# The same steps in another order on five engines: a four-layer graph network over 32 batches

## The reference

```
h = relu(layernorm(x)); x = x + L0(h, adj)   # 8-head attention with q=k=v, then an MLP 256-1024-256 with gelu
h = relu(layernorm(x)); x = x + L1(h, adj)   # graph attention, 4 heads: weights exp(leaky_relu(s_i + t_j)), masked
h = relu(layernorm(x)); x = x + L2(h, adj)   # the same form, other weights
h = relu(layernorm(x)); x = x + L3(h, adj)   # 4-head attention with q, k, v and output projection, masked, diagonal open
```

## Time and profile before

| what | us |
|---|---|
| median of three runs (lowest, highest) | 4239.26 (4238.15, 4240.60) |
| the profiled execution itself | 4241.92 |
| its span, from the first to the last instruction | 4240.1 |
| PE busy | 4042.6 (95%) |
| DVE busy | 3223.4 (76%) |
| ACT busy | 2166.5 (51%) |
| POOL busy | 408.3 (10%) |
| mean granted TensorE clock, share of full | 0.988 |

### The profile page before, as it was taken

The page is one execution under the profiler, slowest core; times in us unless marked ns, Lnnn a source line. Parts: engine busy times, 40 slices in busy tenths (PEclk is TensorE's granted clock), DMA queues, the critical chain, the costliest instruction groups (busy, mean ns, idle before and its releaser), DMA issues.

```text
span 4240.1 us, 58963 instructions
## 1 busy us (share of the span) xinstructions
PE 4042.6 (95%) x22884; PEld 1929.7 (46%) x22884; DVE 3223.4 (76%) x6473; ACT 2166.5 (51%) x3361; POOL 408.3 (10%) x469
## 2 busy tenths in 40 slices
PE   5799999999999999999999999999999999999997
PEld 1344444444444444444444444444444444444443
DVE  5677778877778877777877777877778877788854
ACT  3454555544555554555544555544555544555532
POOL 0001011101011101110100110100110100110100
PEclk9999999999999999999999999999999999999998
DMA  3111111111111111111111111112111111211000
GB/s 99 29 42 50 56 37 49 34 53 51 56 36 51 31 53 52 56 36 51 31 52 54 56 35 51 31 51 56 56 32 54 31 51 56 56 31 46 21 31 31
DMA packets 212311, 193.90 MB, mean 46 GB/s; under 512 B 144448, under 2 KB 179008, under 8 KB 203584
## 3 DMA queue, kind: packets, MB, share of 16 engines
q1 hardware_dynamic: 212032, 190.12, 15.3%
HBM read 138.95 MB, written 17.56 MB: 37 GB/s over the span
## 4 chain that ended last, share of the span: by engine, by line
PE 90%; DVE 5%; ACT 4%; DMA 1%; issue 1%; SPq 0%; POOL 0%; POOLq 0%; ACTq 0%; DVEq 0%
PE O L477 12%; PE M L425 11%; PE M L438 10%; PE S L358 6%; PE S L524 6%; PE O L371 6%; PE M L491 6%; PE O L540 6%; PE M L449 6%; PE O L481 5%; PE M L502 3%; PE M L416 3%; PE M L582 3%; PE O L382 2%; ACT PP L625 2%; PE M L398 2%
## 5 line engine op out<-in xcount | busy, mean ns | idle before, releaser
L1014 DVE SCALAR_TENSOR_TENSOR PG<-g,tcg,mT 128x512 f32<-128x512 f32 x1024 | 691.2, 742 | 33.1 <-PE O L481 21.4
L625 ACT ACTIVATE PP<-S,reach 128x1024 f32<-128x1024 f32 x512 | 542.6, 1111 | 318.8 <-PE O L371 114.5
L906 DVE TENSOR_TENSOR PP<-PP,mT 128x1024 f32<-128x1024 f32 x512 | 597.3, 1218 | 16.5 <-ACT PP L625 16.0
L477 PE MATMUL O<-PG,V 128*32 128x512 f32 x4096 | 550.9, 602 | 18.5 <-DVE PG L1014 17.0
L425 PE MATMUL M<-hT,W 128*128 128x512 f32 x1024 | 460.6, 603 | 3.1 <-ACT hT L660 2.8
L438 PE MATMUL M<-W,H 128*128 128x256 f32 x2048 | 459.7, 378 | 0.0
L438 PEld LDWEIGHTS M<-W,H 128*128 128x128 f32 x2048 | 377.3, 189 | 71.7 <-issue 10.6
L1126 POOL TENSOR_SCALAR ve<-mv 128x4 f32<-128x4 f32 x192 | 97.8, 509 | 3197.4 <-DVE mv L864 3197.4
L358 PE MATMUL S<-hT 32*128 32x512 f32 x2048 | 301.3, 658 | 30.8 <-ACT PP L625 29.4
L739 ACT ACTIVATE PP<-S,sh 128x1024 f32<-128x1024 f32 x256 | 272.1, 1118 | 87.5 <-DVE Q L916 49.0
L603 ACT ACTIVATE V<-z,nb,rs 128x256 f32<-128x256 f32 x128 | 76.6, 602 | 467.4 <-DVE nb L896 467.4
(11 more groups left out here) (136 smaller groups left out, 5608.5 us busy)
## 6 DMA issues: line engine op xcount, KB each, us to landing
g<-t_rows SPq DMA_DIRECT2D x64, 1024.0 KB, 4.7
adj<-adj_in SPq DMA_DIRECT2D x32, 1024.0 KB, 5.5
x<-x_in SPq DMA_DIRECT2D x32, 512.0 KB, 4.0
z<-t_rows SPq DMA_DIRECT2D x64, 256.0 KB, 4.0
out<-x SPq DMA_DIRECT2D x32, 512.0 KB, 2.9
W<-w_in SPq DMA_DIRECT2D x1, 3072.0 KB, 13.0
mT<-z SPq DMA_TRANSPOSE x128, 2.5
m<-V SPq DMA_TRANSPOSE x128, 2.5
```

The source lines that it names most:

```text
L477: e.matmul(k.O[0][r:r + 32, :], s.V[:, jt, 64 * hh + 32 * v:64 * hh + 32 * v + 32], p[:, u, :], start=(jt == 0), stop=(jt == NT - 1))
L625: e.activation(p[:, 2 * pair:2 * pair + 2, :], k.S[:, 2 * pair:2 * pair + 2, :], ACT.Exp, bias=k.reach[:, 7:8], scale=SC0).then_inc(k.e0.s ...
L906: e.tensor_tensor(p[:, 2 * pair:2 * pair + 2, :], p[:, 2 * pair:2 * pair + 2, :], s.mT[:, jt:jt + 1, :].to_broadcast([128, 2, N]), ALU.mul ...
L1014: e.scalar_tensor_tensor(out=p[:, u, :], in0=s.T[hh], scalar=s.tcg[:, 1, hh, jt:jt + 1], in1=s.mT[:, jt, :], op0=ALU.max, op1=ALU.mult).th ...
```

## The change

All five lists are replaced. Each list still holds the same steps for the same batches, each once; no step is changed. Where the loop is cut differs: on PE the 28 steps from `b2r(·,0,2)` to `w2(·,3)`, which stood at the head of a pass, stand at the end of the pass before, with batch numbers shifted by one, so the sequence through that cut is as it was. Besides that, steps trade places. The diff, cut to the places spoken of below (the batch numbers of the removed and added lines differ by the shift):

```diff
--- before.py
+++ after.py
         do.tt(b3, 3, 0)
+        do.sc0(b1, 2)
         do.tt(b3, 3, 1)
-        do.sc0(b1, 2)
         do.b2r(b2, 1, 0)
-        do.b2r(b2, 1, 1)
         do.pv0(b1, 0)
         do.pv0(b1, 1)
+        do.b2r(b2, 1, 1)
+        do.b2r(b2, 1, 2)
         do.dn0(b1, 0)
-        do.b2r(b2, 1, 2)
         do.b2r(b2, 1, 3)
         do.sc0(b1, 3)
-        do.pv0(b1, 2)
         do.qk(b3, 0)
         do.qk(b3, 1)
         do.sc0(b1, 4)
+        do.pv0(b1, 2)
         do.pv0(b1, 3)
...
         do.dn0(b1, 1)
+        do.pv0(b1, 4)
         do.qk(b3, 3)
         do.vp(b3, 0)
         do.sc0(b1, 6)
-        do.pv0(b1, 4)
         do.sq3(b3, 0)
...
         do.sc3(b3, 0)
+        do.vp(b3, 1)
         do.tt(b2, 2, 0)
+        do.pv0(b1, 7)
+        do.dn0(b1, 3)
         do.tt(b2, 2, 1)
-        do.pv0(b1, 7)
-        do.vp(b3, 1)
-        do.dn0(b1, 3)
         do.sc3(b3, 1)
...
 def scalar_program(do):
...
+        do.vp(b3, 1)
         do.tt(b2, 2, 0)
-        do.tt(b2, 2, 1)
         do.sc3(b3, 0)
         do.out0(b1, 1)
-        do.vp(b3, 1)
+        do.tt(b2, 2, 1)
         do.sc3(b3, 1)
-        do.ln0(b0, 0)
         do.sc3(b3, 2)
...
+        do.w1(b1, 7)
+        do.ln0(b0, 0)
+        do.out3(b3, 1)
+        do.ln0(b0, 1)
+        do.ln0(b0, 2)
...
 def vector_program(do):
...
-        do.masks(b1, 1)
-        do.resid0(b2)
-        do.bst(b1, 1, 0)
-        do.bst(b1, 1, 1)
-        do.diag(b1)
...
-        do.zb(b1)
...
         do.wo(b4, 0)
+        do.diag(b1)
         do.wo(b4, 1)
...
         do.rc(b2, 1, 0)
+        do.b2r(b2, 1, 0)
         do.rc(b2, 1, 1)
-        do.b2r(b2, 1, 0)
         do.b2r(b2, 1, 1)
...
+        do.pa0(b1, 3)
+        do.sh3(b3)
+        do.zb(b1)
+        do.sc3(b3, 0)
...
+        do.sc3(b3, 1)
+        do.bst(b1, 2, 0)
+        do.pa3(b3, 0)
...
+        do.fin(b1, 0, 3)
+        do.pa3(b3, 1)
+        do.bag(b1, 2, 2)
+        do.bst(b1, 2, 3)
+        do.bag(b1, 2, 3)
+        do.pj(b2, 2, 0)
+        do.pj(b2, 2, 1)
+        do.sc3(b3, 2)
+        do.pj(b2, 2, 2)
+        do.nb(b1, 2)
...
 def gpsimd_program(do):
...
+        do.rs(b2, 0)
+        do.rs(b3, 3)
+        do.rs(b2, 1)
         do.gmax(b3, 1)
         do.rs(b4, 5)
         do.rs(b3, 4)
-        do.rs(b1, 0)
         do.rs(b2, 2)
         do.gmax(b3, 2)
-        do.rs(b1, 1)
-        do.rs(b2, 3)
...
 def sync_program(do):
...
-        do.loada(b1)
-        do.trow(b4, 2)
-        do.tbc(b4, 2)
...
+        do.trow(b3, 2)
+        do.tbc(b3, 2)
+        do.masks_t(b1, 0)
+        do.masks_t(b1, 1)
...
+        do.store(b4)
+        do.load(b0)
+        do.loada(b0)
```

More of the change, by code:

```diff
@@ L1382, in scalar_program @@
         do.lnz(b3, 3, 2)
+        do.qt(b1, 1)
         do.lnz(b3, 3, 3)
@@ L1390, in scalar_program @@
         do.sc0(b1, 4)
+        do.out0(b1, 0)
         do.qk(b3, 1)
@@ L1393, in scalar_program @@
         do.sc0(b1, 5)
-        do.out0(b1, 0)
+        do.qk(b3, 3)
         do.sq3(b3, 0)
-        do.lnz(b2, 2, 0)
-        do.qk(b3, 3)
-        do.lnz(b2, 2, 1)
         do.vp(b3, 0)
@@ L1529, in vector_program @@
         do.pa0(b1, 1)
-        do.bst(b2, 4, 1)
-        do.bag(b2, 4, 0)
+        do.fin(b2, 1, 1)
+        do.bst(b0, 0, 0)
+        do.bst(b0, 0, 1)
+        do.bst(b2, 4, 0)
         do.fin(b2, 1, 2)
         do.fin(b2, 1, 3)
-        do.bst(b0, 0, 0)
+        do.sc0(b1, 4)
+        do.bst(b2, 4, 1)
         do.bst(b2, 4, 2)
+        do.bag(b2, 4, 0)
         do.bag(b2, 4, 1)
@@ L1539, in vector_program @@
         do.bag(b2, 4, 3)
-        do.bag(b0, 0, 0)
[L1541 to L1544, removed]
+        do.sc0(b1, 5)
+        do.pa0(b1, 2)
+        do.sq3(b3, 0)
+        do.sc0(b1, 6)
+        do.nb(b2, 4)
+        do.sq3(b3, 1)
+        do.sc0(b1, 7)
+        do.pa0(b1, 3)
+        do.sh3(b3)
+        do.zb(b1)
+        do.sc3(b3, 0)
+        do.rc(b1, 0, 0)
+        do.b2r(b1, 0, 0)
+        do.rc(b1, 0, 1)
+        do.bag(b0, 0, 0)
+        do.fin(b1, 0, 0)
@@ new lines, in vector_program @@
+        do.sc3(b3, 1)
+        do.bst(b1, 2, 0)
+        do.pa3(b3, 0)
+        do.b2r(b1, 0, 1)
+        do.rc(b1, 0, 2)
+        do.bag(b1, 2, 0)
+        do.b2r(b1, 0, 2)
+        do.fin(b1, 0, 1)
+        do.fin(b1, 0, 2)
+        do.bst(b1, 2, 1)
+        do.rc(b1, 0, 3)
+        do.bag(b1, 2, 1)
+        do.b2r(b1, 0, 3)
+        do.bst(b1, 2, 2)
+        do.fin(b1, 0, 3)
[3 more added lines that the diff above has]
+        do.bag(b1, 2, 3)
+        do.pj(b2, 2, 0)
@@ L1545, in vector_program @@
+        do.pj(b2, 2, 1)
+        do.sc3(b3, 2)
+        do.pj(b2, 2, 2)
+        do.nb(b1, 2)
+        do.prep_b(b1)
+        do.prep_w(b1)
         do.bst(b0, 0, 2)
         do.bag(b0, 0, 1)
-        do.pa0(b1, 2)
+        do.pj(b2, 2, 3)
+        do.gmax(b2, 2)
+        do.sc3(b3, 3)
+        do.gprep(b2, 2)
+        do.pa3(b3, 2)
+        do.pa3(b3, 3)
+        do.masks(b0, 0)
+        do.bst(b0, 0, 3)
         do.bag(b0, 0, 2)
-        do.bst(b0, 0, 3)
-        do.sq3(b3, 0)
-        do.sc0(b1, 6)
@@ L1552, in vector_program @@
         do.bag(b0, 0, 3)
[L1553 to L1561, removed]
-        do.nb(b0, 0)
[L1563 to L1572, removed]
@@ L1575, in gpsimd_program @@
-def gpsimd_program(do):
-    for it in range(1, NB + 4):
-        b1, b2, b3, b4 = it - 1, it - 2, it - 3, it - 4
+        do.resid0(b1)
+        do.nb(b0, 0)
+        do.w2(b1, 0)
+        do.masks(b0, 1)
+        do.bst(b0, 1, 0)
+        do.gvals(b2, 2)
+        do.bag(b0, 1, 0)
+        do.bst(b1, 3, 0)
+        do.w2(b1, 1)
+        do.gw(b2, 2, 0)
+        do.bag(b1, 3, 0)
+        do.w2(b1, 2)
+        do.bst(b1, 3, 1)
+        do.bst(b0, 1, 1)
+        do.bst(b1, 3, 2)
+        do.bst(b0, 1, 2)
@@ L1579, in gpsimd_program @@
+        do.bag(b0, 1, 1)
+        do.bag(b0, 1, 2)
+        do.bag(b1, 3, 1)
+        do.bst(b0, 1, 3)
+        do.bag(b0, 1, 3)
+        do.w2(b1, 3)
+        do.bst(b1, 3, 3)
+        do.bag(b1, 3, 2)
+def gpsimd_program(do):
+    for it in range(2, NB + 4):
+        b2, b3, b4 = it - 2, it - 3, it - 4
+        do.rs(b2, 0)
+        do.rs(b3, 3)
+        do.rs(b2, 1)
         do.gmax(b3, 1)
```

192 lines of the change are left out of this document (69 added, 123 removed).

## The result

The changed kernel takes 4251.24 us (median of 9 runs, 4248.17 to 4255.44) beside 4240.37 (9 runs, 4236.98 to 4243.18) for the kernel before: ratio 1.0026, 95% interval 1.0016 to 1.0036. It is slower by 0.26%, 10.9 us. The forecast, 4235 and most likely no change, fell on the wrong side. The time lies inside the range of 4223 to 4257, and the mechanism that made it is rival A.

The account below looks back on a forecast made before the run. PE, busy 3427 of 3500 us, was taken as the bound. Passes -3, head -3.7 and tail +2.8 took the profiled 4241.9 to 4238.0; for the median, 4239.3 - 3.9 gave 4235, range 4223 to 4257.

Parts of the forecast that it names:

- rival A: Side chain: rs(b,2) starts into a long DVE instruction or the bag is later; about +0.6 us a pass, 4256; chance 0.22.
- (e): Side chain from the MLP's statistics through rs and gelu to grow: bag 1.0 us later, cost 0, bounds 0 and +0.6.
- The slack of 0.3 us: At grow on PE: the gelu of w1(b,0) ends at 2120.76 and frees M0 at 2121.12, leaving 0.3 us.
- (a): PE, b2r(b,1,2) ahead of dn0(b,0): PE waits for DVE to free M0, sc0(b,3) later, +0.2 us a pass.
- rival B: DVE reaches pa0(b,0) sooner, so the wait at b2r(b,1,2) doesn't bite: -0.4 us a pass, 4227; chance 0.23.
- The signal itself: Profile sign: PE waits for DVE L935 at the third b2r of layer 1, not for ACT at sc0(b,3).
- (b): PE, pv0(b,2) moved behind two qk: its 0.22 us wait for the mask goes, -0.2 us a pass.
- (c): PE, equal forms become neighbours: three new pairs at 0.11 us each, two tt parted, -0.2 us a pass in all.
- (d): PE waits at b2r(b,0,1) because ACT's out0(b,1) delays freeing M1: +0.1 us a pass, between 0 and 0.3.
- (f): zb, diag, the masks, ln0 and the SP swaps lie beside other work; no cost booked.
- Head: Start of batch 0: statistics ready earlier without diag, -3.3 us, and zb off the path, -0.4; sum -3.7 (-5 to 0).
- Tail: ACT does vp(b,1) ahead of sc3(b,0): last batch +1.9 us, the batch before 0.9; sum +2.8 (0 to +4).

Follow-up runs that it names:

- x1: Changed kernel with one VectorE step, pa3(b,1), moved back behind bag(b,2,3): 4226.3 us, 127.21 us a pass, ratio 0.9963 to the kernel before.
- x2: Changed kernel with two short VectorE steps (0.5 us together) moved up ahead of the masks' product sc3(b,2): 4233.0 us, ratio 0.9981 to the kernel before.
- x4: Changed kernel with the epsilon addition for the MLP's normalisation taken from POOL to VectorE: 4227.5 us, ratio 0.9967 to the kernel before.
- y1: As x1, with dn0(b,0) ahead of b2r(b,1,2) on PE again: 4230.2 us, 127.44 us a pass, ratio 0.9974 to the kernel before.
- y3: Kernel before, with only b2r(b,1,2) moved ahead of dn0(b,0) on PE: 4242.0 us, 127.71 us a pass, ratio 1.0005.
- z2: As x1, with pv0(b,4) on PE back behind sc0(b,6): 4229.9 us, 127.34 us a pass, ratio 0.9966 to the kernel before.
- z1: As x1, with ACT's copy of vp(b,1) behind out0 again in the last batch only: 4220.7 us, ratio 0.9948 to the kernel before.
- y4: As y1, with ACT's copy of vp(b,1) behind out0 again in the last batch only: 4230.1 us, ratio 0.9973 to the kernel before.
- x3: Kernel before, with only pa3(b,1) on VectorE moved ahead of the last bst and two bag: 4271.7 us, 128.74 us a pass, ratio 1.0072.

## Why the prediction was wrong

**The step that failed is (e)**, the side chain, which I booked at 0 with +0.6 as its upper bound. It costs 0.45 us a pass measured against the kernel before, and 0.88 against the same kernel without it (x1). Term by term, counted from w2:

- The bag was to end at 2109.2, 104.1 us behind w2. It ended at 103.6, half a microsecond better than feared and half a microsecond later than before.
- From there to the end of rs I took 2.4 us (0.1 + 0.3 + 2.0); it was 3.3, as in the earlier trace rows. This is the mis-sized term: +0.9. The two short copies behind the bag are no cover: DVE's product starts 0.04 us behind the bag's end (2111.77), POOL's addition 0.09. x2, with 0.5 us more of short work, got the 0.23 us addition. On this the rule that I had cited from SBUF — State Buffer of the Trainium skill, section Who interferes with whom, holds: the trace agrees that POOL's 0.2 us addition lasts as long as DVE's product with two SBUF inputs that starts just ahead of it (1.25 beside 1.2 us). I had named the rule, and then bet on the order of two starts 0.05 us apart. The rows bear it out in one direction only: POOL is held by DVE, but the products of DVE (L906, L916, L1044, L1055) last 1.18 to 1.23 us throughout the profiles of before, after, x2 and x4, also in x2, where POOL's power starts 0.05 us ahead of the product and takes 2.14 us.
- rs ended at 106.9. My own point of decision for rival A, 2111.8, is 106.7. The rival's price of 0.6 was near: 0.45 measured. By its own rows it should have been 0.73 (2121.85 - 2121.12); I took off PE's gain of 0.1, which a pass that the chain sets doesn't get. That it came out near is in part luck, since the bag was 0.5 us earlier than in the rival.
- The reduction started 6.00 us behind rs and not 5.81; over 31 batches it is 5.7 to 6.1 before (mean 5.88) and 5.8 to 6.3 after (mean 5.99).
- The slack of 0.3 us was too large and was taken against the old PE. Where PE waits for it, grow starts 0.14 us behind the end of the gelu; before, that end lies at 115.75 and grow starts at 116.04 (means of 26 full passes), so the slack was 0.15. And PE itself comes to w1(b,0) 0.5 us earlier, and a slack shrinks by what the main path gains: an unchanged chain would already have kept PE waiting some 0.35 us.
- The sum: bag +0.5, from there to the end of rs as before, reduction +0.1, less the slack of 0.15. That is the 0.45 of a pass.

**(a)** was booked at +0.2 and is -0.2 in the new order (y1 against x1; in the changed kernel itself the side chain hides it). Two errors: pa0(b,0) started 57.06 us behind w2 and not 57.34, since DVE's new list twice puts a fin between reciprocal and product, whose starts stand 0.21 us apart without one, and so hides a short wait; that was rival B's argument, and it came true beside A's. And the 0.2 would not have stayed, as y3 shows: pv0(b,2)'s wait swallows it. The signal itself (PE waits for L935, not for ACT) came as written.

**(b) and (c)** were booked at -0.2 each. At qk(b,2), behind pv0(b,2) and pv0(b,3), PE is 0.41 us ahead of before, against 0.05 at sc0(b,3), and the further pairs bring 0.1 each; z2 confirms the size of a pair on its own. Together about -0.5: a little better than booked, though only one pair was tested alone. **(d)**, +0.1, was 0.05. **(f)** held, none of those steps shows a wait on PE.

So PE alone gained 0.5 us a pass up to w1(b,0), where I had 0.1. That is rival B's size, and the chain took all of it and 0.45 more. x1 is what the forecast would have been with B right and (e) right: 127.21, where B said 127.2.

**Head**: -3.7 booked, -5.3 seen at w2(0,0), of which 1.6 is the start of L595, which scatters; diag was booked at -3.3 and measured -3.0. It didn't last: the first four passes gave 3.4 us back, of which about 1.4 (3 x 0.45) go with the wait at grow, which stands in the last three of them. The rest is not explained. **Tail**: the swap was booked at +1.9 for the last batch and cost 1.8 (z1, y4: -1.8 when undone). The 0.9 for the batch before it was not tested. I took 2.8 for the whole tail and -2.2 came, because the clock of a stretch full of gaps isn't a term of my sum. In x1 the same stretch is slow again (its qk takes 8.83 us), and between the changed kernel, x1 and x2, whose lists hardly differ there, w2(31,0) to the end is 190.7, 196.0 and 190.9 us. Both kinds come with the old lists as well. What decides between them stays open; no run tests it, and each kernel has only one profile.

The numbers: +12.2 us in 27 passes where the sum had -3 in 29 is more than the whole error of 12 us between 4238.0 and the 4250.0 profiled; head, first passes and tail together took 3 us of it back.

## What to carry to other kernels

When an order is changed, price side chains that end on the main path first, and take their slack against the new main path, less all that this gains; one 1.13 us step of other work ahead of a chain's first link cost 1.1 us a pass here (x3), and moving it back gave 0.88 (x1). A bound worked out from a row elsewhere (a 0.23 us addition) holds only if its cover is there: write down what the neighbour engine starts within a tenth of a microsecond of it. And before two waits on one path are booked separately, see whether a delay at the first is simply taken off the second.
